# Stage two quantises its rows two tiles in advance, with the gate product on VectorE, and stage one forms four column sums and one row tile later

## The chip, the cores and the metric

The kernel runs on one core of one Trainium2 chip. A core has five engines that run side by side, each through its own list of instructions in a fixed order, and that meet only through semaphores: TensorE (PE in the profile; its weight loads are PEld), VectorE (DVE), ScalarE (ACT), GpSimd (POOL) and SyncE (SP, which here only issues transfers). The metric is the device time of one execution in microseconds (us). The kernel before takes 1054.46 us, the median of three runs that lie between 1053.47 and 1055.18 us.

## The reference, cut to what matters

An attention-like product and a SwiGLU feed-forward block, both on quantised numbers, over x of 2 x 1024 rows of 2048 features:

```python
x = x + matmul(fake_quant(layernorm(x)), fake_quant(ctx))     # 8 bits, one scale and zero point each
h = layernorm(x).astype(bfloat16)
qg, sg = dynamic_quant(h * inv_gate)     # scale of a row = max|.| / 127, then round to int8
qu, su = dynamic_quant(h * inv_up)
gate = (qg @ w_gate.T) * sg * s_gate     # w_gate, w_up: 1024 x 2048
up   = (qu @ w_up.T) * su * s_up
inter = clip(silu(gate) * up, -10, 10).astype(bfloat16)
qi, si = dynamic_quant(inter * inv_inter)
out = x + (qi @ w_down.T) * si * s_down  # w_down: 2048 x 1024
```

The zero points of the first product are brought in by sums: the column sums of the quantised context, times a constant, are added to every row (a column bias), and row sums of x come in at the very end. Each weight matrix is held as two fp16 halves, high and low, so that every product of the feed-forward block is two matmuls.

## The kernel before, in words

The 2048 rows are 16 row tiles of 128. There are three stages, and all matmuls are 128 x 128 by 128 x 512.

**Stage one** (line L1079) has 64 groups, each of one row tile m and one chunk of 512 context columns: 16 matmuls into one of five PSUM banks. There are four chunks for each of two batches, so eight chunks, 0 to 7, each of four quarters; the quarters are the 32 context transfers. A quarter is loaded into one of three staging buffers (ACT issues the load, L439), rounded to uint8 (VectorE, L762; the last quarter of each chunk ScalarE, L446), and cast to fp16 (ScalarE, L455; the last one GpSimd, L698). VectorE adds the four quarters of a chunk in fp16 (`col_add`, L779 and L782), TensorE sums the result over the partitions with a matrix of ones (`col_sum`, L1048, four matmuls), and ScalarE writes the bias (`col_bias`, L476). VectorE empties each group's bank into the row tile (`evacuate`, L808), GpSimd adds the column bias (`adjust`, L691), and SyncE stores the finished tile to a scratch tensor (`store_x2`). Row tiles 8 to 15 take over the memory of earlier ones: tile 13 is loaded when the last quarter, number 31, has been cast by GpSimd, and tile 15 when tile 8 has been stored. A row tile m is normalised and quantised (`ln1_stats` L789, `quantise_x` L462 and L470) and turned by a DMA transpose (`transpose_x`, L266) before its first group. The tables `adds_at`, `colsum_after`, `colbias_at`, `stats_at`, `quantise_at` say at which group number each engine does which of these; each engine walks through the 64 group numbers in order.

**Stage two** (L1099) has 64 jobs, one for each row tile t and one of four parts p: 0 and 2 are gate, 1 and 3 are up, 512 columns each; a job is 32 matmuls. A part's weights come in four granules of 1 MB, one transfer each. ScalarE takes their absolute sums (`w_abs`, L493), VectorE makes a power-of-two scale of them (`w_scale`, from L814), ScalarE writes the high half (`w_hi`, L507) and VectorE the low half (`w_lo`, L849), in turns. A job of part p waits for all low halves of that part. Of the first two row tiles a part is run for both before the next half's parts follow (tile 0 gate and up, tile 1 gate and up of the first 512 columns, then part 2 of both, then part 3 of both); the last two row tiles run half by half. For each row tile SyncE loads the 128 rows back (`load_x2`), VectorE takes their statistics (`ln2_stats`, L789), GpSimd makes the row scalars (`ln2_scalars`, from L663), ScalarE writes h in bf16 (`h_bf16`, L517), GpSimd multiplies h by inv_gate (`smooth_gate`, L672) and by inv_up (`smooth_up`, L684), VectorE finds the row maximum and rounds to int8 (`quantise`, L870 and L861), ScalarE casts to fp16 (`cast_q`, L529), and SyncE turns the result by a DMA transpose (`transpose_q`, L295) into one of two buffers for even and odd tiles. The results are emptied by VectorE (`evac_gate` L883, `evac_up` L891 to L898) with the silu on ScalarE between them (L535), then quantised for the third stage (`quant_inter`, L905 and on, `cast_qi` L539).

**Stage three** (L1111) has 64 products of 16 matmuls, one for each row tile and one of four output chunks, whose weights are parts 4 to 7 of two granules each; `down` (L920, L925) empties them.

The order is written by hand, engine by engine. In the middle of stage two VectorE's order for row tile t is this, one tile in advance:

```python
ln2_stats(t + 1)
evac_gate(t, 0)
quantise(0, t + 1)
evac_up(t, 0)
evac_gate(t, 1)
quantise(1, t + 1)
evac_up(t, 1)
quant_inter(t)
```

## Time and profile before

| what | value |
|---|---|
| median of three runs | 1054.46 us |
| the profiled execution, whole | 1058.52 us |
| its span on the core | 1056.8 us |
| TensorE busy | 939.6 us, 89% |
| VectorE busy | 666.1 us, 63% |
| ScalarE busy | 360.4 us, 34% |
| GpSimd busy | 295.3 us, 28% |

One profiled execution is the source of every row below. The part of the span in which an engine's instructions run is its busy time; what counts for the end is where TensorE, the busiest, does nothing, and what it then waits for. In rows of the timeline the first number is the start in the span, the second the length, and what stands in brackets is the idle time before the instruction and what ended it.

### The profile page before, as it was taken

To read this page: it belongs to the slowest core of one execution; us is meant where nothing else is said; L and a number is where in the kernel's file an instruction comes from. 1 tells how busy PE (TensorE), PEld (TensorE's weight loads), DVE (VectorE), ACT (ScalarE), POOL (GpSimd) and SP (SyncE) were. 2 spreads that over 40 slices of the span, in tenths; PEclk is the share of its full clock that TensorE was granted. 3 is DMA by queue.
4 is the path that set the end of the run, shared out by engine and by line. 5 is a ranking of instruction groups with operands and counts; after the bars stand their busy time and mean duration, and the time that the engine had idled before them with its cause. 6 is when DMAs were issued, how large, how long until landed. Compare 5 with 4: busy or idle time off the path is not lost.

```text
span 1056.8 us, 11253 instructions
## 1 busy us (share of the span) xinstructions
PE 939.6 (89%) x4192; PEld 416.0 (39%) x4192; DVE 666.1 (63%) x1006; ACT 360.4 (34%) x281; POOL 295.3 (28%) x256
## 2 busy tenths in 40 slices
PE   1689886799696778899999999999959989999998
PEld 1333332344242333344444444444424434444443
DVE  5469374657396777666777777777566694444443
ACT  4735456456445652222222333333226520000000
POOL 2226655364356021333333323223420000000000
PEclk9799988899897888899999999999989989999999
DMA  9665797976848803231333333333349630994112
GB/s 356 240 268 199 245 368 227 350 271 204 289 165 274 282 21 78 79 71 54 89 90 90 90 90 90 90 90 90 80 125 336 255 110 1 314 347 136 80 80 79
DMA packets 131686, 179.52 MB, mean 170 GB/s; under 512 B 111024, under 2 KB 111024, under 8 KB 113968
## 3 DMA queue, kind: packets, MB, share of 16 engines
q1 hardware_dynamic: 126848, 144.72, 43.8%
q10 hardware_dynamic: 4752, 34.08, 8.1%
q8 instruction: 33, 0.54, 0.2%
q0 software_dynamic: 32, 0.00, 0.1%
q14 instruction: 21, 0.17, 0.1%
HBM read 113.77 MB, written 37.75 MB: 143 GB/s over the span
## 4 chain that ended last, share of the span: by engine, by line
PE 58%; DVE 12%; issue 10%; DMA 8%; POOL 5%; ACT 5%; ACTq 0%; SPq 0%; DVEq 0%; POOLq 0%
PE ps L1099 36%; PE ps L1111 19%; DVE w_slots L849 5%; POOL x_tile L691 3%; PE ps L1079 3%; DMA ctx_stage<-in_ctx 2%; DVE small_operands L789 2%; DMA q1T<-x_q 2%; ACT x_i L462 1%; DMA w_raw<-in_w_gu 1%; DMA x_tile<-in_x 1%; DMA w_raw<-in_w_dn 1%; DVE ctx_u L762 1%; POOL ctx_slot L698 1%; DMA qT_odd<-q_f 1%
## 5 line engine op out<-in xcount | busy, mean ns | idle before, releaser
L1079 PE MATMUL ps<-ctx_slot,q1T 128*128 128x512 f16 x1024 | 237.2, 394 | 22.5 <-DMA q1T<-x_q 11.1
L1099 PE MATMUL ps<-w_slots,qT_even 128*128 128x512 f16 x1024 | 233.5, 391 | 21.1 <-issue 8.6
L1099 PE MATMUL ps<-w_slots,qT_odd 128*128 128x512 f16 x1024 | 231.9, 389 | 21.8 <-issue 19.7
L1111 PE MATMUL ps<-w_slots,qiT 128*128 128x512 f16 x1024 | 224.1, 382 | 4.1 <-DVE gate_and_up L891 4.1
L1079 PEld LDWEIGHTS ps<-ctx_slot,q1T 128*128 128x128 f16 x1024 | 102.7, 101 | 154.4 <-issue 16.8
L1099 PEld LDWEIGHTS ps<-w_slots,qT_even 128*128 128x128 f16 x1024 | 102.0, 100 | 151.8 <-issue 32.2
L1099 PEld LDWEIGHTS ps<-w_slots,qT_odd 128*128 128x128 f16 x1024 | 101.8, 100 | 151.2 <-issue 35.2
L1111 PEld LDWEIGHTS ps<-w_slots,qiT 128*128 128x128 f16 x1024 | 100.8, 99 | 127.3 <-DVE w_slots L849 4.6
L529 ACT ACTIVATE q_f<-q_i 128x2048 f16<-128x2048 int8 x32 | 61.1, 1910 | 195.0 <-DVE q_i L861 190.1
L920 DVE SCALAR_TENSOR_TENSOR down_tmp<-ps,small_operands,down_scales_b 128x512 f32<-128x512 f32 x64 | 48.0, 750 | 99.3 <-PE ps L1111 99.2
L870 DVE TENSOR_REDUCE small_operands<-x_and_xs 128x1 f32<-128x2048 f32 x19 | 43.4, 2284 | 105.9 <-POOL x_and_xs L672 102.3
L691 POOL TENSOR_TENSOR x_tile<-x_tile,col_bias 128x512 f32<-128x512 f32 x64 | 92.5, 1467 | 39.4 <-DVE x_tile L808 39.4
L808 DVE SCALAR_TENSOR_TENSOR x_tile<-ps,small_operands,x_tile 128x512 f32<-128x512 f32 x64 | 46.6, 734 | 57.1 <-PE ps L1079 56.9
L849 DVE SCALAR_TENSOR_TENSOR w_slots<-w_raw,small_operands,w_slots 128x1024 f16<-128x1024 f32 x48 | 68.7, 1430 | 13.9 <-ACT w_slots L507 10.4
L663 POOL TENSOR_SCALAR small_operands<-small_operands 128x1 f32<-128x1 f32 x16 | 4.0, 251 | 261.4 <-DVE small_operands L792 261.4
L672 POOL TENSOR_TENSOR x_and_xs<-h_bf,inv_gate_b 128x2048 f32<-128x2048 bf16 x16 | 65.5, 4092 | 39.2 <-ACT h_bf L517 39.2
L455 ACT ACTIVATE ctx_slot<-ctx_u 128x2048 f16<-128x2048 uint8 x24 | 45.5, 1905 | 74.4 <-DVE ctx_u L762 48.3
L507 ACT ACTIVATE w_slots<-w_raw,small_operands 128x1024 f16<-128x1024 f32 x48 | 52.4, 1139 | 30.2 <-DVE small_operands L832 17.4
L684 POOL TENSOR_TENSOR xs_up<-h_bf,inv_up_b 128x2048 f32<-128x2048 bf16 x13 | 53.2, 4096 | 0.0
L925 DVE SCALAR_TENSOR_TENSOR x_tile<-x_tile,small_operands,down_tmp 128x512 f32<-128x512 f32 x64 | 48.1, 752 | 2.3
L517 ACT ACTIVATE h_bf<-x_and_xs,small_operands 128x2048 bf16<-128x2048 f32 x15 | 31.4, 2093 | 53.0 <-POOL small_operands L666 53.0
L789 DVE BATCH_NORM_STATS2 small_operands<-x_and_xs 128x6 f32<-128x512 f32 x60 | 37.1, 681 | 8.7 <-DMA x_and_xs<-x_scratch 8.3
(91 smaller groups left out, 679.1 us busy)
## 6 DMA issues: line engine op xcount, KB each, us to landing
ctx_stage<-in_ctx ACTq DMA_DIRECT2D x32, 1024.0 KB, 8.1
x_scratch<-x_tile SPq DMA_DIRECT2D x16, 1024.0 KB, 5.0
w_raw<-in_w_gu SPq DMA_DIRECT2D x16, 1024.0 KB, 9.1
x_tile<-x_scratch SPq DMA_DIRECT2D x16, 1024.0 KB, 8.4
x_tile<-in_x SPq DMA_DIRECT2D x15, 1024.0 KB, 9.4
x_and_xs<-x_scratch SPq DMA_DIRECT2D x15, 1024.0 KB, 5.8
out_x<-x_tile SPq DMA_DIRECT2D x15, 1024.0 KB, 5.1
w_raw<-in_w_dn SPq DMA_DIRECT2D x8, 1024.0 KB, 9.2
```

Of the source, the lines that this page charges most:

```text
L507: nc.scalar.activation(hi[:, a * 2 * CW:(a + 1) * 2 * CW], raw[:, raw_unit(p, g), a * 2 * CW:(a + 1) * 2 * CW], ACT.Identity, bias=0.0, sc ...
L529: nc.scalar.activation(q16[:, :], q8[:, :], ACT.Copy).then_inc(q16_ready[which], 1)
L672: nc.gpsimd.tensor_tensor(bufA[:, :], hb[:, :], invg_b[:, :], ALU.mult).then_inc(xs_ready[0], 1)
L684: nc.gpsimd.tensor_tensor(dst[:, :], hb[:, :], invu_b[:, :], ALU.mult).then_inc(xs_ready[1], 1)
L691: nc.gpsimd.tensor_tensor(part, part, colb[:, j % 4, :], ALU.add).then_inc(adj_done, 1)
L789: ins = nc.vector.bn_stats(stats[:, 6 * c:6 * c + 6], src[:, c * CW:(c + 1) * CW])
L849: nc.vector.scalar_tensor_tensor(lo[:, cols], raw[:, raw_unit(p, g), cols], wsc[:, p:p + 1], hi[:, cols], ALU.mult, ALU.subtract).then_inc ...
L920: nc.vector.scalar_tensor_tensor(tmp[:, i % 2, :], ps[:, bank(S3 + i), :], si[:, t:t + 1], swd_b[:, c, :], ALU.mult, ALU.mult).then_inc(ev ...
L925: nc.vector.scalar_tensor_tensor(part, part, rterm[:, t:t + 1], tmp[:, i % 2, :], ALU.add, ALU.add).then_inc(res_done, 1)
L1079: last = nc.tensor.matmul(ps[:, bank(g), :], q1T[m][:, k, :], ctx_s[j % 4][:, k, :], start=(k == 0), stop=(k == KT - 1))
L1099: last = nc.tensor.matmul(ps[:, bank(S2 + i), :], qT[t % 2][:, which, k, :], wsl[:, unit(p, k // 4), hl, k % 4, :], start=(k == 0 and hl = ...
L1111: last = nc.tensor.matmul(ps[:, bank(S3 + i), :], qiT[t % 8][:, k, :], wsl[:, unit(4 + c, k // 4), hl, k % 4, :], start=(k == 0 and hl == ...
```

## The change

Four things change. The column sums of chunks 4 to 7 stand three groups later on TensorE, and VectorE makes the three additions of each of these chunks together instead of one after each quarter. The order of the groups of row tiles 13, 14 and 15 is another one:

```diff
-        groups += [(12, c) for c in range(NCH)] + [(13 + g % 3, g // 3) for g in range(12)]
+        groups += [(12, c) for c in range(NCH)]
+        for half in ((0, 1), (2, 3)):
+            groups += [(m, c) for c in half for m in (13, 14)] + [(15, c) for c in half]
...
-        adds_at.update({g + 1: (q,) for g, q in quad_at.items() if g >= 20})
+        adds_at.update({4 * j + 9: (4 * j + 1, 4 * j + 2, 4 * j + 3) for j in range(4, 8)})
...
-        colsum_after = {6: 0, 9: 1, 11: 2, 14: 3, 25: 4, 29: 5, 33: 6, 37: 7}
-        colbias_at = {7: 0, 10: 1, 12: 2, 15: 3, 26: 4, 30: 5, 34: 6, 38: 7}
+        colsum_after = {6: 0, 9: 1, 11: 2, 14: 3, 28: 4, 32: 5, 36: 6, 40: 7}
+        colbias_at = {7: 0, 10: 1, 12: 2, 15: 3, 29: 4, 33: 5, 37: 6, 41: 7}
```

On TensorE, in the groups of the second half of the first batch and the beginning of the second, where `q1T` is a turned row tile, `ctx_slot` a context chunk and `ones` the matrix of a column sum, this stands before:

```order
L1079 MATMUL ps<-ctx_slot2_53,q1T5_79 128x512 x16
L1048 MATMUL ps<-ctx_colacc_93,ones_133 128x512 x4
L1079 MATMUL ps<-ctx_slot2_53,q1T6_80 128x512 x16
L1079 MATMUL ps<-ctx_slot2_53,q1T7_81 128x512 x16
L1079 MATMUL ps<-ctx_slot3_54,q1T4_78 128x512 x16
L1079 MATMUL ps<-ctx_slot3_54,q1T5_79 128x512 x16
L1048 MATMUL ps<-ctx_colacc_93,ones_133 128x512 x4
```

and this after:

```order
L1084 MATMUL ps<-ctx_slot2_53,q1T5_79 128x512 x16
L1084 MATMUL ps<-ctx_slot2_53,q1T6_80 128x512 x16
L1084 MATMUL ps<-ctx_slot2_53,q1T7_81 128x512 x16
L1084 MATMUL ps<-ctx_slot3_54,q1T4_78 128x512 x16
L1053 MATMUL ps<-ctx_colacc_93,ones_133 128x512 x4
L1084 MATMUL ps<-ctx_slot3_54,q1T5_79 128x512 x16
```

The column sum of chunk 4 has moved behind three more groups; those of chunks 5, 6 and 7 move in the same way. At the end of stage one TensorE has this before, in which `q1T15` is row tile 15:

```order
L1079 MATMUL ps<-ctx_slot0_51,q1T13_87 128x512 x16
L1079 MATMUL ps<-ctx_slot0_51,q1T14_88 128x512 x16
L1079 MATMUL ps<-ctx_slot0_51,q1T15_89 128x512 x16
L1079 MATMUL ps<-ctx_slot1_52,q1T13_87 128x512 x16
L1079 MATMUL ps<-ctx_slot1_52,q1T14_88 128x512 x16
```

and this after:

```order
L1084 MATMUL ps<-ctx_slot0_51,q1T13_87 128x512 x16
L1084 MATMUL ps<-ctx_slot0_51,q1T14_88 128x512 x16
L1084 MATMUL ps<-ctx_slot1_52,q1T13_87 128x512 x16
L1084 MATMUL ps<-ctx_slot1_52,q1T14_88 128x512 x16
L1084 MATMUL ps<-ctx_slot0_51,q1T15_89 128x512 x16
```

Row tile 15 comes in for the first time as the 57th group instead of the 55th.

Third, the gate product moves from GpSimd to VectorE, where it stands at the head of `quantise(0, t)`; GpSimd keeps the up product:

```diff
             for t in range(2, NT):
                 ln2_scalars(t)
-                smooth_gate(t)
                 smooth_up(t)
```

Fourth, from row tile 2 on stage two quantises row tile t + 2 while t is computed, where it was t + 1. VectorE's list gains the product and the loop changes; at the beginning the fourth low half of part 1 goes behind the first quantisation, and at the end the last emptying of stage two goes ahead of the weights of parts 6 and 7:

```diff
+            def smooth_gate(t):
+                dve.wait_ge(hb_ready, t + 1)
+                if t == 0:
+                    dve.wait_ge(invg_in, 16)
+                if t in (1, 2):
+                    dve.wait_ge(q8_written, q8_at["u", t - 1] + 1)
+                nc.vector.tensor_tensor(bufA[:, :], hb[:, :], invg_b[:, :], ALU.mult).then_inc(xs_ready[0], 1)
+
             def quantise(which, t):
+                if which == 0:
+                    smooth_gate(t)
...
-                if 56 <= g < 60:
-                    w_lo(1, g - 56)
+                if g in (56, 57, 58, 60):
+                    w_lo(1, {56: 0, 57: 1, 58: 2, 60: 3}[g])
...
-                if g == 60:
+                if g == 59:
                     quantise(0, 0)
...
-            for t in range(2, NT - 2):
-                ln2_stats(t + 1)
+            for t in range(2, NT - 1):
                 evac_gate(t, 0)
-                quantise(0, t + 1)
+                if t + 2 < NT:
+                    ln2_stats(t + 2)
                 evac_up(t, 0)
-                evac_gate(t, 1)
-                quantise(1, t + 1)
-                if t == NT - 3:
-                    ln2_stats(NT - 1)
-                    quantise(0, NT - 1)
-                evac_up(t, 1)
-                quant_inter(t)
-            evac_gate(NT - 2, 0)
-            quantise(1, NT - 1)
-            evac_up(NT - 2, 0)
+                if t + 2 < NT:
+                    evac_gate(t, 1)
+                    quantise(0, t + 2)
+                    evac_up(t, 1)
+                    quant_inter(t)
+                    quantise(1, t + 2)
             evac_gate(NT - 1, 0)
             evac_up(NT - 1, 0)
...
             evac_up(NT - 2, 1)
             quant_inter(NT - 2)
+            evac_gate(NT - 1, 1)
+            evac_up(NT - 1, 1)
+            quant_inter(NT - 1)
             w_scale(6)
             sw_scale(6)
             w_lo(6, 0)
             w_lo(6, 1)
-            evac_gate(NT - 1, 1)
-            w_scale(7)
-            sw_scale(7)
-            w_lo(7, 0)
-            w_lo(7, 1)
-            evac_up(NT - 1, 1)
-            quant_inter(NT - 1)
             dve.wait_ge(rterm_ready, 1)
             for i in range(G1):
+                if i == 6:
+                    w_scale(7)
+                    sw_scale(7)
+                    w_lo(7, 0)
+                    w_lo(7, 1)
                 down(i)
```

ScalarE follows, with the casts of the next rows ahead of the silu:

```diff
-            for t in range(2, NT - 2):
-                h_bf16(t + 1)
-                silu(t, 0)
-                cast_q(0, t + 1)
-                silu(t, 1)
-                cast_q(1, t + 1)
...
+            for t in range(3, NT):
+                cast_q(0, t)
+                cast_qi(t - 2)
+                cast_q(1, t)
+                silu(t - 1, 0)
+                if t + 1 < NT:
+                    h_bf16(t + 1)
+                    silu(t - 1, 1)
```

and so does SyncE:

```diff
-            for t in range(2, NT - 2):
-                store_qi(t - 1)
-                transpose_q(0, t + 1)
-                load_x2(t + 2)
-                transpose_q(1, t + 1)
+            for t in range(3, NT):
+                if t + 1 < NT:
+                    load_x2(t + 1)
+                transpose_q(0, t)
+                store_qi(t - 2)
+                if t + 1 < NT:
+                    transpose_q(1, t)
```

Here is a turn of VectorE's loop up to the first emptying of an up job. `x_and_xs` is the buffer of the loaded rows and of the gate product, `q_i` the int8 result, L883 and L891 the emptying of gate and up. Before:

```order
L883 SCALAR_TENSOR_TENSOR gate_and_up<-ps,small_operands,gate_up_scales_b 128x512
L870 TENSOR_REDUCE small_operands<-x_and_xs 128x1
L871 TENSOR_SCALAR small_operands<-small_operands 128x1
L874 COPY small_operands<-small_operands 128x1
L856 RECIPROCAL small_operands<-small_operands 128x1
L861 TENSOR_SCALAR q_i_104<-x_and_xs,small_operands 128x2048
L891 SCALAR_TENSOR_TENSOR gate_and_up<-ps,small_operands,gate_up_scales_b 128x512
```

After:

```order
L886 SCALAR_TENSOR_TENSOR gate_and_up<-ps,small_operands,gate_up_scales_b 128x512
L862 TENSOR_TENSOR x_and_xs<-h_bf_103,inv_gate_b 128x2048
L873 TENSOR_REDUCE small_operands<-x_and_xs 128x1
L874 TENSOR_SCALAR small_operands<-small_operands 128x1
L877 COPY small_operands<-small_operands 128x1
L849 RECIPROCAL small_operands<-small_operands 128x1
L854 TENSOR_SCALAR q_i_104<-x_and_xs,small_operands 128x2048
L894 SCALAR_TENSOR_TENSOR gate_and_up<-ps,small_operands,gate_up_scales_b 128x512
```

The product (L862) is new on VectorE, and the emptying ahead of it is now that of part 2 of the tile, where it was part 0.

At the beginning of stage two the weights of parts 2 and 3 are prepared in another order. On ScalarE, where `abs_junk` marks an absolute sum, `w_slots` a high half (two instructions to a granule) and `gate_and_up` a silu, this stands before:

```order
L493 ACTIVATE abs_junk_late_112,small_operands_135<-w_raw_49 128x2048
L507 ACTIVATE w_slots_50<-w_raw_49,small_operands_135 128x1024 x8
L493 ACTIVATE abs_junk_late_112,small_operands_135<-w_raw_49 128x2048 x3
L535 ACTIVATE gate_and_up_106<-gate_and_up_106 128x512
L507 ACTIVATE w_slots_50<-w_raw_49,small_operands_135 128x1024 x8
```

and this after:

```order
L508 ACTIVATE w_slots_50<-w_raw_49,small_operands_135 128x1024 x4
L536 ACTIVATE gate_and_up_106<-gate_and_up_106 128x512
L494 ACTIVATE abs_junk_late_112,small_operands_135<-w_raw_49 128x2048
L508 ACTIVATE w_slots_50<-w_raw_49,small_operands_135 128x1024 x2
L494 ACTIVATE abs_junk_late_112,small_operands_135<-w_raw_49 128x2048
L508 ACTIVATE w_slots_50<-w_raw_49,small_operands_135 128x1024 x2
```

Part 2's eight high halves stood together; now its last four have two absolute sums of part 3 among them. In this beginning SyncE stores row tiles 13 to 15 after more of the weight loads and after the transpose of the first up rows, and loads part 3 in the order of its granules.

## Rows read from the trace of the kernel before

**Rows 1.** Page, part 1: busy time of the engines, share, instructions.

```profile
PE 939.6 (89%) x4192; PEld 416.0 (39%) x4192; DVE 666.1 (63%) x1006; ACT 360.4 (34%) x281; POOL 295.3 (28%) x256
```

**Rows 2.** What TensorE waited for: total us, times, longest.

```profile
PE ps L1048 <- DVE ctx_colacc L782: 21.9, 6, 8.1
```

**Rows 3.** Timeline of TensorE in stage one: start, length, operation, wait before.

```profile
151.28 1.89 PE L1048 MATMUL ps<-ctx_colacc,ones 128*128 128x512 f16 x4 [4.74 <-DVE ctx_colacc L782]
...
176.24 1.89 PE L1048 MATMUL ps<-ctx_colacc,ones 128*128 128x512 f16 x4 [8.09 <-DVE ctx_colacc L782]
...
197.88 1.89 PE L1048 MATMUL ps<-ctx_colacc,ones 128*128 128x512 f16 x4 [5.29 <-DVE ctx_colacc L782]
...
216.86 1.04 PE L1048 MATMUL ps<-ctx_colacc,ones 128*128 128x512 f16 x4 [1.52 <-DVE ctx_colacc L782]
217.74 55.42 PE L1079 MATMUL ps<-ctx_slot,q1T 128*128 128x512 f16 x256
281.21 36.62 PE L1079 MATMUL ps<-ctx_slot,q1T 128*128 128x512 f16 x160 [8.06 <-DMA q1T<-x_q]
```

**Rows 4.** Timelines of VectorE, GpSimd and ScalarE in stage one.

```profile
174.96 1.23 DVE L782 TENSOR_TENSOR ctx_colacc<-ctx_colacc,ctx_slot 128x2048 f16<-128x2048 f16 x1 [4.06 <-POOL ctx_slot L698]
...
265.50 2.46 DVE L789 BATCH_NORM_STATS2 small_operands<-x_tile 128x6 f32<-128x512 f32 x4
...
212.60 1.90 POOL L698 TENSOR_SCALAR ctx_slot<-ctx_u 128x2048 f16<-128x2048 uint8 x1 [8.31 <-ACT ctx_u L446]
...
225.41 1.91 ACT L493 ACTIVATE abs_junk_early<-w_raw 128x2048 uint8<-128x2048 f32 x1 [12.90 <-DMA w_raw<-in_w_gu]
```

**Rows 5.** Windows: PE, PEld, DVE, ACT, POOL busy, clock, DMA share, GB/s.

```profile
120.00:210.00 90.00, 69.68 (x293) 29.88 (x294) 51.34 (x60) 45.69 (x30) 41.64 (x39) 0.89 0.94 320
```

**Rows 6.** Timeline of TensorE at the beginning of stage two.

```profile
323.99 9.77 PE L1099 MATMUL ps<-w_slots,qT_even 128*128 128x512 f16 x32 [6.17 <-DMA qT_even<-q_f]
337.80 9.69 PE L1099 MATMUL ps<-w_slots,qT_even 128*128 128x512 f16 x32 [4.04 <-issue]
351.58 9.63 PE L1099 MATMUL ps<-w_slots,qT_odd 128*128 128x512 f16 x32 [4.09 <-issue]
...
392.14 9.84 PE L1099 MATMUL ps<-w_slots,qT_even 128*128 128x512 f16 x32 [6.28 <-DVE w_slots L849]
...
420.32 23.20 PE L1099 MATMUL ps<-w_slots,qT_even 128*128 128x512 f16 x96 [4.54 <-issue]
446.82 30.51 PE L1099 MATMUL ps<-w_slots,qT_odd 128*128 128x512 f16 x128 [3.30 <-issue]
477.17 27.79 PE L1099 MATMUL ps<-w_slots,qT_even 128*128 128x512 f16 x128
```

**Rows 7.** Timelines of VectorE, GpSimd and ScalarE at the beginning of stage two.

```profile
306.66 6.39 DVE L849 SCALAR_TENSOR_TENSOR w_slots<-w_raw,small_operands,w_slots 128x1024 f16<-128x1024 f32 x2 [1.47 <-ACT w_slots L507]
...
381.12 10.95 DVE L849 SCALAR_TENSOR_TENSOR w_slots<-w_raw,small_operands,w_slots 128x1024 f16<-128x1024 f32 x8
...
448.67 1.23 DVE L905 TENSOR_TENSOR gate_and_up<-inter_even,inv_inter_b 128x1024 f32<-128x1024 bf16 x1
...
305.66 4.10 POOL L672 TENSOR_TENSOR x_and_xs<-h_bf,inv_gate_b 128x2048 f32<-128x2048 bf16 x1
...
368.84 1.91 ACT L493 ACTIVATE abs_junk_late<-w_raw 128x2048 uint8<-128x2048 f32 x1
```

**Rows 8.** Window in the middle of stage two, and VectorE there.

```profile
500.00:600.00 100.00, 100.00 (x463) 44.86 (x462) 73.18 (x110) 30.41 (x23) 28.95 (x22) 1.00 0.38 95
...
521.15 2.29 DVE L870 TENSOR_REDUCE small_operands<-x_and_xs 128x1 f32<-128x2048 f32 x1 [7.20 <-POOL x_and_xs L672]
```

**Rows 9.** Timeline of TensorE at the end of stage two.

```profile
779.72 8.90 PE L1099 MATMUL ps<-w_slots,qT_odd 128*128 128x512 f16 x32 [11.05 <-issue]
789.87 7.07 PE L1099 MATMUL ps<-w_slots,qT_odd 128*128 128x512 f16 x32 [1.25 <-issue]
...
852.88 199.79 PE L1111 MATMUL ps<-w_slots,qiT 128*128 128x512 f16 x912 [4.14 <-DVE gate_and_up L891]
```

More of the change, by code:

```diff
@@ L581, in _ @@
             cast_q(0, 1)
+            silu(0, 0)
             w_abs(2, 2)
@@ L623, in _ @@
             cast_qi(NT - 2)
[L624 to L632 removed]
+            w_abs(6, 0)
+            w_abs(6, 1)
+            silu(NT - 1, 1)
+            w_abs(7, 0)
+            w_abs(7, 1)
+            cast_qi(NT - 1)
+            for p in (6, 7):
+                w_hi(p, 0)
+                w_hi(p, 1)
         @block.gpsimd
@@ L719, in _ @@
                     adjust(n)
-            smooth_gate(1)
             for n in adjust_at[G1]:
```

95 lines of the change are left out of this document (41 added, 54 removed).

## The prediction

> **What bounds the kernel now.** I read the shares of the engines first: TensorE is busy 939.6 of 1056.8 us, no other engine over 666.1 [rows 1]. So the time is TensorE's work plus 117 us in which it stands still, and some further work done at the lower of its two clock levels after it stood. Then I read its timeline for every stop, and at each one who ends it.
>
> In the middle of stage two there is none: a window of 100 us is 100 us busy at a granted clock of 1.00, that is 2.4 GHz [rows 8], and one row tile of four jobs takes 27.79 us [rows 6]. The same holds in stage three. Whatever the change does to other engines there is worth nothing unless it makes them slower than 27.8 us for a row tile. The stops lie in four places. In stage one TensorE waits before four column sums, 4.74, 8.09, 5.29 and 1.52 us [rows 3], most of the 21.9 us that it waits for these sums in all [rows 2], and later 8.06 us for the transpose of row tile 15 [rows 3]. At the beginning of stage two come waits of 6.17, 4.04, 4.09, 6.28, 4.54 and 3.30 us [rows 6]; those marked "issue" end when a DMA transpose of quantised rows lands, the one with w_slots when the low halves of a part are ready. At the end of it come 11.05 and 1.25 us for the last transposes, and in stage three 4.14 us for the last emptying, which stands on VectorE behind weight work [rows 9].
>
> A stop costs more than its length. 32 matmuls take 27.79 / 4 = 6.95 us at 2.4 GHz; behind a stop they take 9.77, 9.69 or 9.84 [rows 6], since part of them runs at 1.2 GHz. That is 2.7 to 2.9 us on top of each stop of 3 us or more.
>
> **The change part by part.** A positive number is time saved.
>
> *A. Column sums, 10.* Starts of these four sums lie 25.0, 21.6 and 19.0 us apart [rows 3], while four groups take 4 x 55.42 / 16 = 13.9. So the stream of context quarters, not the place of the sum, sets this pace, and a sum moved back by three groups only lets TensorE run ahead by 10.4 us. What follows does not hang on TensorE: GpSimd's cast of the last quarter at 212.60 releases a row tile load and the first weights, for which ScalarE then waits 12.90 us [rows 4]. If the stream keeps its pace, TensorE will give its lead back by waiting for banks, because VectorE's emptying stands behind the scale of part 0's weights. So only what the stream itself gains counts. It gains this: before, VectorE waited 4.06 us with the addition of a chunk's last quarter (1.23) while the next chunk's first rounding stood behind it [rows 4]. Now the additions come one group later, behind that rounding. That is 5.3 us at one chunk boundary; I take the same at the next, 10.6, and call it 10. Bounds: 0, if the stream is held elsewhere, and 19.6, the four waits. The transfers leave some room, but not much: 0.94 of the DMA engines' time between 120 and 210 us, at 320 GB/s [rows 5].
>
> *B. Row tile 15, 6.9.* Its first group comes two groups later, 2 x 3.46 us. Since its statistics (265.50 before, [rows 4]) stay tied to the chain of A, the end of stage one comes 6.9 nearer to that chain. The wait itself shrinks by less, because TensorE also arrives with what is left of its lead from A, some 5 us; about 6 of it stay. Bounds 0 and 8.1.
>
> *C. First transpose of stage two, 3.5.* Row tile 0 is loaded when row tile 15's first group is done, now with 7 groups behind it instead of 9, which costs 6.9 of cover. Against that, the chain loses the fourth low half of part 1, 6.39 us ahead of the first maximum [rows 7], and the gate product gets shorter: VectorE makes 128x1024 of the same types in 1.23 us, so twice that, 2.4, against 4.10 on GpSimd [rows 7]. The gap becomes 6.17 + 6.9 - 6.4 - 1.7 = 5.0. VectorE also comes to the statistics earlier, as the scale of part 1 no longer has to wait behind a late emptying; for this I take half of the 5.0, so 6.17 - 2.5, about 3.5 saved. Bounds -2 and 6.2.
>
> *D. The rest of the beginning, 8.* From the first job at 323.99 to the fifth row tile at 477.17 TensorE needs 153.2 us for 16 jobs of 6.95, so 42 are lost. With rows ready two tiles ahead the last two waits go, 4.54 + 3.30, and their low clock (23.20 - 3 x 6.95 = 2.4 and 30.51 - 27.79 = 2.7): 12.9. Half of the 4.09 goes as well, 2.0, because the second gate rows no longer queue behind stores. But part 2's last two granules now have two absolute sums of 1.91 [rows 7] among them on ScalarE, and VectorE's low halves, and with them part 2's first job, come 3.8 us later; a stop there makes the clock fall, 2.8 more. 12.9 + 2.0 - 6.6 = 8.3, taken as 8. What now is late next at this place is the low halves of parts 2 and 3, not the rows. Bounds -7 (only the new waits) and 42; I take the value at the low end because the weight work (eight low halves alone 10.95 us [rows 7]) stays.
>
> *E. The end of stage two, 19.6.* The last rows are quantised a whole row tile before TensorE asks for them, so 11.05 goes, and with it the low clock, 8.90 - 6.95 = 2.0. With the last emptying ahead of parts 6 and 7, the 4.14 go, and the low clock behind them: 199.79 - 912 x 55.42 / 256 = 2.4. The 1.25 I leave out. Weights of parts 4 and 5 have five jobs, 35 us, from their load on, and stage three then comes to part 6 after 12 products and to part 7 after 18, so these hide. Bounds 0 and 21.
>
> *F. VectorE's new load, 0.* Per row tile it is busy 73.18 x 27.79 / 100 = 20.3 us, and waited 7.20 us for the gate product [rows 8]. The wait goes, 2.4 come in: 22.7, under 27.8. TensorE's work covers this; the cover is 5.1 us per row tile.
>
> Here is what speaks against F. While GpSimd made a product of 4.10 us, two low halves took VectorE 6.39 us; eight undisturbed ones take 10.95, so 1.4 each [rows 7], and the two lost 3.7. Both products of a row tile are now released by the same h, so the gate product can start just behind GpSimd's and lose up to 4.1. The Trainium skill, "SBUF — State Buffer", section "SBUF: two separate sides", says the same as a rule: a VectorE instruction with two SBUF inputs and a GpSimd instruction share one port pair, whichever starts first holds it throughout, the other is blocked entirely. The trace agrees with 6.39 against 2.7. By this the load is 22.7 + 4.1 = 26.8, still under 27.8, and the sum stays.
>
> Sum: 10 + 6.9 + 3.5 + 8 + 19.6 = 48.0 us. Against the profiled execution's own 1058.5 that is 1010.5; that execution is 4.1 above the median of the runs, so I predict 1054.5 - 48.0 = 1006.5 us.
>
> **The rivals.** *The stream keeps its pace* (A is 0): the 0.94 of DMA time [rows 5] speaks for it, since transposes and stores share these engines; the waiting rounding behind 4.06 us speaks against. 1016.5 us. *The weights decide the beginning* (D is -7): parts 2 and 3 are scaled later than now, and every later low half too; the wait of 6.28 for w_slots shows that they already do once [rows 6]. 1021.5 us. *The end keeps its stop* (E is 0): transposes come in time, but TensorE reaches stage three before part 4 is ready; against it stand the five jobs of cover. 1026 us. *VectorE becomes the bound of stage two, slower than before*: with colliding products it is at 26.8 us, and if its roundings and inter products are blocked by the up product as well, or each silu is waited for, it passes 27.8. It pays per row tile, in twelve of them: at 33 us, 12 x 5.2 = 62 us, so 1006.5 + 62 = 1068. It only outweighs the gain from 27.8 + 48 / 12 = 31.8 us on, 5 above the collided load, for which no row speaks.
>
> **How the numbers follow.** Differences under 0.2%, about 2 us, can't be told from none here. Forecast 0.64, with a range of its own from 998 to 1014; stream 0.16; weights 0.12; end 0.04; VectorE 0.04. Only the last ends slower, and nothing lies near zero, but 0.02 I keep for gains and new waits that cancel: faster 0.94, same 0.02, slower 0.04. The range goes down to 992, where A is nearly 20 and D some 13, and up to 1026, which takes in the first three rivals.
>
> **What would show it.** A: GpSimd's last cast of a context quarter near 202 instead of 212.6; no stops before column sums over 4 us; instead short waits of TensorE for emptied banks near row tile 12. B and C: TensorE's first job of stage two near 303, a wait of some 6 us left at row tile 15 and one under 4 before the first job. D: waits for w_slots before parts 2 and 3 of about 8 us, then none from row tile 2 on. E: no stop over 1 us from there to the last matmul, and the first product of stage three about 35 us after row tile 15's first job. F: VectorE about 80% busy in the middle with TensorE at 100%. The forecast is wrong if GpSimd's last cast hardly moves, if a stop appears in every row tile of stage two, or if stage three waits for low halves.

## The result and the profile after

The changed kernel takes 1012.67 us (median of 4 runs, 1008.1 to 1020.4) against 1054.82 for the kernel before (1053.47 to 1059.44); the ratio is 0.9598, 95% interval 0.9564 to 0.9632. It is 42 us faster, where 48 were forecast. The profiled execution took 1015.74 us with a span of 1014.0, 42.8 under the span before. The ratios here and below leave out slow executions, of which there were two: 1024.24 us (the changed kernel, taken again) and 1023.65 us (both edits to ScalarE's order together).

Part 1 of its page answers to [rows 1]: TensorE's busy time falls by 26 us with the same 4192 matmuls, while its mean granted clock rises from 0.950 to 0.976, so less of this work ran at the lower clock. VectorE's busy time rises by 41 us.

```profile
PE 913.8 (90%) x4192; PEld 410.0 (40%) x4192; DVE 707.3 (70%) x1022; ACT 361.4 (36%) x281; POOL 252.5 (25%) x240
```

TensorE's timeline of stage one (start, length, operation, wait before) answers to [rows 3]. L1053 are the column sums of chunks 4 to 7, and the last line begins with row tile 15. The first long run of groups is put ahead here, that of the kernel before (L1079) and then the changed kernel's.

```profile
122.19 24.35 PE L1079 MATMUL ps<-ctx_slot,q1T 128*128 128x512 f16 x112 [2.77 <-DMA q1T<-x_q]
```

```profile
119.06 34.71 PE L1084 MATMUL ps<-ctx_slot,q1T 128*128 128x512 f16 x160 [2.76 <-DMA q1T<-x_q]
153.60 1.03 PE L1053 MATMUL ps<-ctx_colacc,ones 128*128 128x512 f16 x4
...
189.15 1.86 PE L1053 MATMUL ps<-ctx_colacc,ones 128*128 128x512 f16 x4 [20.21 <-ACT col_bias L477]
...
205.70 1.03 PE L1053 MATMUL ps<-ctx_colacc,ones 128*128 128x512 f16 x4
...
220.38 1.03 PE L1053 MATMUL ps<-ctx_colacc,ones 128*128 128x512 f16 x4
221.24 51.96 PE L1084 MATMUL ps<-ctx_slot,q1T 128*128 128x512 f16 x240
278.47 29.39 PE L1084 MATMUL ps<-ctx_slot,q1T 128*128 128x512 f16 x128 [5.27 <-DMA q1T<-x_q]
```

Four stops of together 19.6 us have become one of 20.2. All column sums use one PSUM bank, so col_sum(5) waits until ScalarE has read col_sum(4) out of it (col_bias(4)). GpSimd's and ScalarE's timelines answer to [rows 4]: the stream's last cast came at 208.2 (before 212.6, forecast 202). As the long run of groups began 3.1 us earlier, the stream itself gained only 1.3 of these 4.4 us. ScalarE's first work on the weights comes 14.1 us behind that cast (before 12.8).

```profile
208.21 2.93 POOL L694 TENSOR_SCALAR ctx_slot<-ctx_u 128x2048 f16<-128x2048 uint8 x1 [3.57 <-ACT ctx_u L447]
...
222.32 1.91 ACT L494 ACTIVATE abs_junk_early<-w_raw 128x2048 uint8<-128x2048 f32 x1 [13.63 <-DMA w_raw<-in_w_gu]
```

TensorE's timeline at the beginning and end of stage two answers to [rows 6, 9]. The waits for late rows at row tiles 2 and 3 fell from 4.54 and 3.30 to 1.11 and 0.66, the one for part 3's low halves grew from 6.28 to 9.13, and from row tile 4 on there is no stop at all. A wait of 2.99 for part 2's low halves is new.

```profile
312.67 8.63 PE L1104 MATMUL ps<-w_slots,qT_even 128*128 128x512 f16 x32 [4.81 <-DVE x_tile L801]
326.65 8.46 PE L1104 MATMUL ps<-w_slots,qT_even 128*128 128x512 f16 x32 [5.36 <-issue]
338.09 7.07 PE L1104 MATMUL ps<-w_slots,qT_odd 128*128 128x512 f16 x32 [2.97 <-issue]
...
361.26 7.08 PE L1104 MATMUL ps<-w_slots,qT_even 128*128 128x512 f16 x32 [2.99 <-DVE w_slots L842]
...
384.37 8.63 PE L1104 MATMUL ps<-w_slots,qT_even 128*128 128x512 f16 x32 [9.13 <-DVE w_slots L842]
...
407.92 20.88 PE L1104 MATMUL ps<-w_slots,qT_even 128*128 128x512 f16 x96 [1.11 <-issue]
429.45 27.93 PE L1104 MATMUL ps<-w_slots,qT_odd 128*128 128x512 f16 x128 [0.66 <-issue]
457.23 27.79 PE L1104 MATMUL ps<-w_slots,qT_even 128*128 128x512 f16 x128
...
733.49 13.98 PE L1104 MATMUL ps<-w_slots,qT_even 128*128 128x512 f16 x64
...
788.74 221.18 PE L1116 MATMUL ps<-w_slots,qiT 128*128 128x512 f16 x1024
```

The window in the middle answers to [rows 8]; VectorE has 84 us of 100 where it had 73.

```profile
500.00:600.00 100.00, 100.00 (x465) 45.32 (x464) 84.08 (x116) 31.75 (x23) 26.29 (x20) 1.00 0.34 89
```

In the kernel before, row tile 14, with which the end of stage two begins, started here:

```profile
754.69 13.97 PE L1099 MATMUL ps<-w_slots,qT_even 128*128 128x512 f16 x64
```

From these rows the 42.8 us split by place. The first long run of groups began at 119.06 and not at 122.19: 3.1, in work that the change does not touch; in the other kernels tried, which share that code, it began between 119.3 and 122.3, so this is chance. From there to the end of stage one (307.86, before 317.83) it took 188.8 for 195.6: 6.8. From there to row tile 4's first job 149.4 for 159.3: 10.0. The ten row tiles 4 to 13 276.3 for 277.5: 1.3. From there to the end 280.5 for 302.1: 21.6.

### The profile page after: what moved, and what is told of

It is laid out like the page before. It is cut to its first block, busy times and chain, and to the rows that moved or that the text cites. A ratio compares the mean times of both kernels' runs of the same rounds, so it can differ in the third digit from the quotient of the medians.

```text
span 1014.0 us, 11256 instructions
## 1 busy us (share of the span) xinstructions
PE 913.8 (90%) x4192; PEld 410.0 (40%) x4192; DVE 707.3 (70%) x1022; ACT 361.4 (36%) x281; POOL 252.5 (25%) x240
## 4 chain that ended last, share of the span: by engine, by line
PE 67%; DMA 11%; DVE 9%; issue 6%; ACT 3%; POOL 2%; SPq 1%; ACTq 0%; DVEq 0%; POOLq 0%
PE ps L1104 40%; PE ps L1116 22%; PE ps L1084 5%; DMA q1T<-x_q 5%; DMA ctx_stage<-in_ctx 2%; DVE w_slots L842 2%; DMA w_raw<-in_w_gu 2%; DVE small_operands L782 2%; DVE ctx_u L755 1%; POOL x_tile L687 1%; DMA small_operands<-in_params 1%; ACT x_q L471 1%; DMA qT_odd<-q_f 1%; SPq L297 1%; DVE small_operands L873 1%
## 5 line engine op out<-in xcount | busy, mean ns | idle before, releaser
L1104 PE MATMUL ps<-w_slots,qT_even 128*128 128x512 f16 x1024 | 227.6, 385 | 23.4 <-DVE w_slots L842 12.1
L1084 PE MATMUL ps<-ctx_slot,q1T 128*128 128x512 f16 x1024 | 231.1, 387 | 18.0 <-DMA q1T<-x_q 8.3
L1104 PE MATMUL ps<-w_slots,qT_odd 128*128 128x512 f16 x1024 | 224.8, 381 | 8.0 <-DVE w_slots L842 4.4
L1116 PE MATMUL ps<-w_slots,qiT 128*128 128x512 f16 x1024 | 221.2, 379 | 0.0
L687 POOL TENSOR_TENSOR x_tile<-x_tile,col_bias 128x512 f32<-128x512 f32 x64 | 101.4, 1608 | 35.6 <-DVE x_tile L801 35.6
L680 POOL TENSOR_TENSOR xs_up<-h_bf,inv_up_b 128x2048 f32<-128x2048 bf16 x13 | 63.7, 4902 | 28.7 <-ACT h_bf L518 28.7
L886 DVE SCALAR_TENSOR_TENSOR gate_and_up<-ps,small_operands,gate_up_scales_b 128x512 f32<-128x512 f32 x32 | 23.9, 748 | 43.0 <-PE ps L1104 42.7
L755 DVE TENSOR_SCALAR ctx_u<-ctx_stage,small_operands 128x2048 uint8<-128x2048 f32 x24 | 38.3, 1595 | 16.3 <-DMA ctx_stage<-in_ctx 11.5
L862 DVE TENSOR_TENSOR x_and_xs<-h_bf,inv_gate_b 128x2048 f32<-128x2048 bf16 x16 | 43.2, 2703 | 8.4 <-ACT h_bf L518 8.4
```

What stands on the lines that cost most here:

```text
L680: nc.gpsimd.tensor_tensor(dst[:, :], hb[:, :], invu_b[:, :], ALU.mult).then_inc(xs_ready[1], 1)
L687: nc.gpsimd.tensor_tensor(part, part, colb[:, j % 4, :], ALU.add).then_inc(adj_done, 1)
L755: nc.vector.tensor_scalar(cu8[:, q % 2, :, :], stage[q % 3][:, :, :], is2[:, 0:1], qp[:, 3:4], ALU.mult, ALU.add).then_inc(c_quant, 1)
L1084: last = nc.tensor.matmul(ps[:, bank(g), :], q1T[m][:, k, :], ctx_s[j % 4][:, k, :], start=(k == 0), stop=(k == KT - 1))
L1104: last = nc.tensor.matmul(ps[:, bank(S2 + i), :], qT[t % 2][:, which, k, :], wsl[:, unit(p, k // 4), hl, k % 4, :], start=(k == 0 and hl = ...
L1116: last = nc.tensor.matmul(ps[:, bank(S3 + i), :], qiT[t % 8][:, k, :], wsl[:, unit(4 + c, k // 4), hl, k % 4, :], start=(k == 0 and hl == ...
```

## The experiments

Each kernel was timed in rounds with the kernel before on the same chip; ratios are to that, and spans and rows are of one profiled execution. "Stage one" is the time from the start of its first long run of groups (near 120 us) to the end of its last.

### The column sums put back

```diff
-        adds_at.update({4 * j + 9: (4 * j + 1, 4 * j + 2, 4 * j + 3) for j in range(4, 8)})
+        adds_at.update({g + 1: (q,) for g, q in quad_at.items() if g >= 20})
-        colsum_after = {..., 28: 4, 32: 5, 36: 6, 40: 7}
+        colsum_after = {..., 25: 4, 29: 5, 33: 6, 37: 7}
```

(colbias_at likewise.) 

> The changed kernel with the three tables of the column sums (when the quarters are added, after which group the sum is taken, when its bias is formed) put back to those of the kernel before. Theory: moving the sums gave nothing, since one stop of 20.2 us before col_sum(5) took the place of four that came to 19.6 us: 1011 to 1015 us (the changed kernel has 1012.7), and the four stops before column sums are back, 4 to 8 us each. Rival, the prediction's first term: the move was worth 10 us and something else ate it: 1021 to 1025 us.

Measured: 1019.06 us, 0.9626 (0.9610 to 0.9643); all its runs between 1018.4 and 1019.2. The four stops are back (4.74, 9.55, 4.64 and 4.91 us):

```profile
148.44 1.89 PE L1053 MATMUL ps<-ctx_colacc,ones 128*128 128x512 f16 x4 [4.74 <-DVE ctx_colacc L775]
...
174.26 1.89 PE L1053 MATMUL ps<-ctx_colacc,ones 128*128 128x512 f16 x4 [9.55 <-DVE ctx_colacc L775]
...
218.93 91.99 PE L1084 MATMUL ps<-ctx_slot,q1T 128*128 128x512 f16 x416
```

That is 3 us behind the changed kernel's 0.9598, with intervals that overlap: over all executions the move is not worth 10 us. The time lies above the 1011 to 1015 expected, but this chip's kernel before is 4 us slower too; by the ratio it would be 1015 us beside the changed kernel's first four. Stage one took 191.6 us, from 119.36 to 310.92.

### The bias earlier, the rounding earlier, both

The first moves col_bias(4) on ScalarE from group 29 to 26, the second changes one number, the third is both.

```diff
+                if g == 26:
+                    col_bias(4)
-        quantise_at = {..., 24: 9, 26: 10, 28: 11, ...}
+        quantise_at = {..., 24: 9, 27: 10, 28: 11, ...}
```

> The changed kernel, ScalarE forms col_bias(4) at group 26 and not at group 29, so that col_sum(5) does not wait for it behind three casts and a row tile. Theory: what holds TensorE there is the context stream and the transposed row tile 11, which landed at 196.1 us, 1.7 us before TensorE came to need it: the one stop of 20.2 us falls apart into a stop of about 10 us (for the sum of chunk 5, whose last quarter is added at 178.6 us) and one of about 7 us (row tile 11), total 1010 to 1013 us. Rival: the wait for the bias alone lost the prediction's 10 us: 1001 to 1005 us and no stop over 10 us left there.

Measured: 1019.53 us (1009.8 to 1022.9), 0.9612 (0.9579 to 0.9645): no gain. The profiled execution (1022.87) had long transposes, 14.2 and 15.3 us for row tiles 8 and 9. In it TensorE's long stop only fell apart, as the theory had it, into the wait for the sum itself and one for row tile 11's transpose:

```profile
184.55 1.89 PE L1055 MATMUL ps<-ctx_colacc,ones 128*128 128x512 f16 x4 [12.25 <-DVE ctx_colacc L777]
...
199.23 8.60 PE L1086 MATMUL ps<-ctx_slot,q1T 128*128 128x512 f16 x32 [4.71 <-DMA q1T<-x_q]
```

So in that execution the wait that I had overlooked is what one sees, and not what bounds.

> The changed kernel, ScalarE rounds the context's quarter 23 before it quantises row tile 10 and not behind it. In the changed kernel the second half of that quantisation waited 7.1 us for the transpose of row tile 9, and the rounding stood behind it. Theory: the rounding starts near 165.5 us (174.5 in the changed kernel), GpSimd's cast and the scalars of row tile 11 with it, row tile 11 lands near 190 us (196.1), col_bias(4) is formed near 183 us (188.3), and the total is 1007 to 1009 us. Rival: the stop belongs to the moved column sums alone, and the order on ScalarE before it is worth nothing: 1011 to 1014 us.

Measured: 1015.9 us (1007.6 to 1018.8), 0.9591 (0.9563 to 0.9619), not told apart from the changed kernel. In the profiled execution (1007.63) the rounding of quarter 23 started at 160.6, the long stop was 11.83 and stage two began at 304.9; but there the transposes of row tiles 8 and 9 had taken 8.3 and 9.3 us, so that execution cannot say what the order did.

> Both edits together: col_bias(4) at group 26, and the rounding of quarter 23 ahead of row tile 10 on ScalarE. Theory (stream and row tile 11 hold TensorE, each edit takes one of two waits that follow one another): the stop before col_sum(5) shrinks to about 4 us, the group of row tile 11 starts near 190 us (197.8 in the changed kernel), total 1004 to 1007 us. Rival (the bias alone): as the kernel with the bias early, 1001 to 1005 us, and the two differ by less than 1 us.

Measured: 1011.72 us (1008.3 to 1023.7), 0.9558 (0.9528 to 0.9589); the interval overlaps the changed kernel's. The sum no longer waits; the transposes of row tiles 10 and 11 do the holding (1.94 and 10.39 us), and the group of tile 11 starts at 190.7, near the 190 expected. Its shortest executions, 1008.3 and 1008.4, are no shorter than the changed kernel's:

```profile
170.21 1.04 PE L1055 MATMUL ps<-ctx_colacc,ones 128*128 128x512 f16 x4 [0.22 <-DVE ctx_colacc L777]
...
176.64 3.63 PE L1086 MATMUL ps<-ctx_slot,q1T 128*128 128x512 f16 x16 [1.94 <-DMA q1T<-x_q]
190.66 9.07 PE L1086 MATMUL ps<-ctx_slot,q1T 128*128 128x512 f16 x32 [10.39 <-DMA q1T<-x_q]
```

### The changed kernel again

> The changed kernel as it is, for a second profile of it and for a time on the same chip as the three beside it. Theory: what differs from execution to execution is how long the transposes of row tiles 8 and 9 take beside the context loads (14.0 and 14.1 us in the first profile): where they take 7 to 10 us, the rounding of quarter 23 starts before 168 us, the stop before col_sum(5) is under 16 us, and stage two begins before 308 us; where they take 14 us, all is as in the first profile (20 us, 312.7 us). Ratio to the kernel before 0.956 to 0.963. Rival: the stop of 20 us is there with short transposes as well.

Measured: 1020.82 us, 0.9605 (0.9555 to 0.9656). With the first four there are ten times of this kernel: four from 1008.1 to 1009.6 and six from 1015.7 to 1024.2. The granted clock does not part them: its means are 0.972 to 0.975 in the four and 0.966 to 0.976 in the six. Below they are called the lower and the upper group. The profiled one (1021.43) belongs to the upper group: the two transposes took 13.8 and 16.0 us, and the stop 22.4.

```profile
192.70 1.87 PE L1053 MATMUL ps<-ctx_colacc,ones 128*128 128x512 f16 x4 [22.43 <-ACT col_bias L477]
...
225.73 51.96 PE L1084 MATMUL ps<-ctx_slot,q1T 128*128 128x512 f16 x240
```

### Only the order of row tiles 13 to 15

The kernel before, with the change's new lines for `groups` alone.

> The kernel before with one edit of the change alone: the order of the groups of row tiles 13 to 15, so that two more groups stand ahead of row tile 15's first. Theory (the prediction's term of 6.9 us): the stop of 8.06 us before row tile 15's first group falls to 0.5 to 2 us, stage one ends 6 to 7 us earlier, and the total falls by 5 to 8 us, ratio 0.992 to 0.995. Rival: stage two's beginning waits for weights and for row tile 0 that come no earlier, and the total falls by less than 2 us, ratio over 0.998.

Measured: 1051.1 us, 0.9929 (0.9905 to 0.9953), 7.5 us (5 to 10) faster. The profiled span, 1051.4, is 5.4 shorter. Stage one takes 187.5 us for 195.6. TensorE then waits 10.00 us for row tile 0's transposed rows, where it had waited 6.17 [rows 6]: about half of stage one's gain is lost again at once, since row tile 0's chain has two groups less in front of it.

```profile
120.36 24.35 PE L1081 MATMUL ps<-ctx_slot,q1T 128*128 128x512 f16 x112 [2.77 <-DMA q1T<-x_q]
...
280.02 27.80 PE L1081 MATMUL ps<-ctx_slot,q1T 128*128 128x512 f16 x128 [1.42 <-DMA q1T<-x_q]
317.82 8.41 PE L1101 MATMUL ps<-w_slots,qT_even 128*128 128x512 f16 x32 [10.00 <-DMA qT_even<-q_f]
```

### The old order at the end of stage two

As before, ScalarE forms part 6's high halves ahead of `silu(NT - 1, 1)` and part 7's behind it, ahead of `cast_qi(NT - 1)`. VectorE empties the last gate job behind part 6's weights and the last up job behind part 7's (VectorE's part of the edit):

```diff
-            evac_gate(NT - 1, 1)
-            evac_up(NT - 1, 1)
-            quant_inter(NT - 1)
             w_scale(6)
             sw_scale(6)
             w_lo(6, 0)
             w_lo(6, 1)
+            evac_gate(NT - 1, 1)
+            w_scale(7)
+            ...
+            evac_up(NT - 1, 1)
+            quant_inter(NT - 1)
```

> The changed kernel with ScalarE's and VectorE's order at the end of stage two put back to the kernel before's (weights of parts 6 and 7 between the last row tiles' emptying), while rows are still quantised two tiles in advance. Theory (the prediction split the end's 19.6 us into 13.05 us from the advance and 6.5 us from this order): 5 to 8 us slower than the changed kernel, ratio 0.964 to 0.970, with a stop of some 4 us before stage three's products. Rival: the advance alone takes all of it, and the time is the changed kernel's within 2 us.

Measured: 1023.66 us, 0.9657 (0.9615 to 0.9698), some 5 us behind the changed kernel on the same chip, with intervals that overlap a little. The rows are sharper: from stage three's first product to the end it took 233.0 us, with the changed kernel 225.3, so this order is worth 7.7. The 11 us stop [rows 9] did not come back; it belongs to the advance.

```profile
811.66 199.13 PE L1115 MATMUL ps<-w_slots,qiT 128*128 128x512 f16 x912 [5.42 <-DVE gate_and_up L894]
```

### The bank of group 60 first

```diff
-                if g in (56, 57, 58, 60):
+                if g in (56, 57, 58, 61):
```

(the last low half of part 1 moves with it.) 

> The changed kernel, VectorE forms the last low half of part 1 (7.0 us beside GpSimd) one group later, so that the bank of group 60 is emptied ahead of it and stage two's first job need not wait for it. Theory: the first job starts 2 us earlier (at its transposed rows' landing), but the second waits for the same quantised up rows as before, so the 2 us become a longer wait there and the time stays: within 1 us of the changed kernel. Rival (the prediction's third term taken as a place on the path): 2 us faster.

Measured: 1008.04 us (1006.7 to 1021.7), 0.9560 (0.9510 to 0.9609). The first job starts 1.7 us behind the end of stage one and not 4.8, but the second waits 8.29 for 5.36, and starts 17.0 us behind that end. In kernels that have the changed kernel's code up to there it was 17.4 (the old end order), 18.7 and 18.8 (the changed kernel's two). By row tile 4's first job the distance from the end of stage one is 148.2, there 148.1, 149.7 and 149.4. So of the first job's 3.1 us at most 1.5 are left at row tile 4; the lower median comes from four of six executions in the lower group.

```profile
301.89 7.07 PE L1104 MATMUL ps<-w_slots,qT_even 128*128 128x512 f16 x32 [1.67 <-DVE w_slots L842]
317.25 9.33 PE L1104 MATMUL ps<-w_slots,qT_even 128*128 128x512 f16 x32 [8.29 <-issue]
```

This kernel's stage one is the changed kernel's, instruction for instruction, up to group 60, and its profiled execution is of the lower group. ScalarE's timelines of the two beside each other show where the groups part. L447 rounds quarters 19 and 23, L471 is the second half of a row tile's quantisation. First the changed kernel, then this one:

```profile
142.13 2.08 ACT L447 ACTIVATE ctx_u<-ctx_stage,small_operands 128x2048 uint8<-128x2048 f32 x1
...
156.37 1.91 ACT L471 ACTIVATE x_q<-x_i 128x2048 f16<-128x2048 int8 x1 [2.39 <-DMA q1T<-x_q]
...
172.56 1.91 ACT L471 ACTIVATE x_q<-x_i 128x2048 f16<-128x2048 int8 x1 [7.08 <-DMA q1T<-x_q]
...
174.47 2.08 ACT L447 ACTIVATE ctx_u<-ctx_stage,small_operands 128x2048 uint8<-128x2048 f32 x1
```

```profile
142.36 2.08 ACT L447 ACTIVATE ctx_u<-ctx_stage,small_operands 128x2048 uint8<-128x2048 f32 x1
...
154.25 1.91 ACT L471 ACTIVATE x_q<-x_i 128x2048 f16<-128x2048 int8 x1
...
165.29 1.91 ACT L471 ACTIVATE x_q<-x_i 128x2048 f16<-128x2048 int8 x1 [3.18 <-DMA q1T<-x_q]
...
167.20 2.08 ACT L447 ACTIVATE ctx_u<-ctx_stage,small_operands 128x2048 uint8<-128x2048 f32 x1
```

Row tile 9 may be written to the one buffer x_q only when row tile 8's transpose has read it, row tile 10 only behind row tile 9's, and the rounding of the stream stands behind both. Windows show the transfers in that time (PE, PEld, DVE, ACT, POOL busy, clock, DMA share, GB/s), again changed kernel first: the DMA engines are as busy in both, and move a third in the execution of the upper group. Most of that lies in four of the seven us: from 152 to 156 the changed kernel moved 81 GB/s, this one 358.

```profile
149.00:156.00 7.00, 7.00 (x35) 3.14 (x33) 6.76 (x10) 3.18 (x2) 6.33 (x6) 1.00 1.19 109
```

```profile
149.00:156.00 7.00, 7.00 (x35) 3.11 (x33) 6.76 (x10) 5.17 (x3) 6.40 (x6) 1.00 1.04 360
```

The other traces agree. Of the eleven profiled executions with the column sums moved, six have a transpose of row tile 8 or 9 that took 13.8 us or more, and their stage one took 188.8 to 193.6 us; in the other five none took over 10.3, and stage one took 178.9 to 183.8. In the three executions profiled with the sums at their old place these transposes took 6.5 to 10.4 us. Whether moving the sums brings the long transposes about is not shown.

### The loads behind the transpose

```diff
-                    if ahead < QUADS and (kq < 2 or ahead % 4 != 2):
+                    if ahead not in (22, 23) and ahead < QUADS and (kq < 2 or ahead % 4 != 2):
                         load_quad(ahead)
...
+                if m == 9:
+                    load_quad(22)
+                    load_quad(23)
                 nc.scalar.activation(xq[:, :], xi8[:, :], ACT.Copy, ...)
```

> The changed kernel, ScalarE issues the loads of the context's quarters 22 and 23 once row tile 8's transpose has landed (it waits there for that anyway) and not 5 us after that transpose was issued. Theory: what parts the executions of the changed kernel, near 1009 and near 1020 us on this chip, is whether row tile 8's transpose takes 8 or 14 us, and it takes 14 only where these loads are issued into it: the transpose takes 7 to 9 us, the rounding of quarter 23 starts 24 to 27 us after that of quarter 19, and five of six times lie between 1005 and 1013 us. Rival: the long transposes come from elsewhere, and the times fall in both groups as before; or the later loads delay the stream as much as they spare it, and all lie near 1014 us.

Measured: 1020.58 us, 0.9641 (0.9611 to 0.9672), all six between 1016.8 and 1023.4. Row tile 8's transpose took 8.6 us as expected; but the loads now met row tile 9's, and it took 16.8 (view of the DMA issues: copies, median us from issue to landing):

```profile
q1T<-x_q SPq DMA_TRANSPOSE x1, 16.8
```

The rounding of quarter 23 came 33.5 us behind that of quarter 19, as in the upper group. The theory is half fallen: without these loads row tile 8's transpose was short, but they met the next one. Loads beside a transpose do not settle it alone either, since with group 60 first the two met as well and it took 8.3 us.

> Four edits together on the changed kernel: the loads of quarters 22 and 23 behind row tile 8's transpose, quarter 23's rounding ahead of row tile 10, col_bias(4) at group 26, and the last low half of part 1 behind the emptying of group 60. Theory: the stream is held by nothing but the loads, stage two starts near 302 us in every execution, 1003 to 1008 us. Rival: TensorE is bound there by row tile 11 and by the weights, which follow the loads, and it is no faster than the kernel with the late loads alone, within 2 us.

Measured: 1019.94 us, 0.9631 (0.9602 to 0.9661): no gain. This kernel has four edits: the loads behind the transpose, the bias earlier, the rounding earlier and the bank of group 60 first. Row tile 9's transpose took 20.4 us, and TensorE, which no longer waits for the bias, waits for row tiles 9, 10 and 11 in turn:

```profile
178.09 6.50 PE L1089 MATMUL ps<-ctx_slot,q1T 128*128 128x512 f16 x16 [4.00 <-DMA q1T<-x_q]
188.03 4.96 PE L1089 MATMUL ps<-ctx_slot,q1T 128*128 128x512 f16 x16 [3.44 <-DMA q1T<-x_q]
198.04 8.53 PE L1089 MATMUL ps<-ctx_slot,q1T 128*128 128x512 f16 x32 [5.05 <-DMA q1T<-x_q]
```

### VectorE's load and the gate product's place

The maximum of the gate rows is taken twice from row tile 3 on:

```diff
+                for _ in range(2 if t >= 3 and which == 0 else 1):
                     link(nc.vector.tensor_reduce(amax, buf[:, :], ...
```

> The changed kernel with the maximum of the gate rows (2.29 us) taken twice from row tile 3 on, so that VectorE has 2.4 us more in each row tile of stage two. Theory (the prediction's sixth term, VectorE has 22.7 us of work in a period of 27.6 us): the period stays 27.6 us, and the time is the changed kernel's within 3 us. Rival: VectorE's order is itself the chain that TensorE follows, and the period grows by 2.4 us, 31 us in all (13 row tiles), 1040 to 1050 us.

Measured: 1019.6 us (1011.1 to 1026.2), 0.9620 (0.9573 to 0.9667), not told apart from the changed kernel. VectorE is at 91 of 100 us, which is 2.0 us more in a row tile, TensorE still at 100, the period still 27.6. Two short stops appear all the same, 3.54 us before row tile 3, where the changed kernel had 0.66, and 1.25 before row tile 15's second job:

```profile
436.07 27.96 PE L1105 MATMUL ps<-w_slots,qT_odd 128*128 128x512 f16 x128 [3.54 <-issue]
```

```profile
500.00:600.00 100.00, 100.00 (x465) 45.35 (x464) 91.18 (x124) 32.48 (x24) 28.07 (x21) 1.00 0.40 95
```

The last kernel gives `smooth_gate` back to GpSimd, ahead of `smooth_up`, and keeps the advance.

> The changed kernel with the gate product back on GpSimd (4.1 us each beside 3.4 us and 2.3 us on VectorE), rows still quantised two tiles in advance. Theory: the place of the product is worth little in the middle, where nothing waits for it, and 2 to 5 us at the beginning of stage two, where the first rows wait for both products in turn: 1 to 6 us slower than the changed kernel, period 27.6 us. Rival: the advance cannot be kept up with both products on GpSimd (8.2 us and the scalars, beside VectorE's use of the same memory), TensorE stops in each row tile, and it is more than 10 us slower.

Measured: 1019.5 us, 0.9642 (0.9604 to 0.9680), some 4 us behind the changed kernel, intervals overlapping. Its period is 27.6 as well, and its way from row tile 4 to the end no longer; but from the end of stage one to row tile 4 it takes 154.1 us for 149.4. The product's new place pays at the beginning of stage two alone.

## Why the prediction was right, and where it was off

The forecast (1006.5, range 992 to 1026) names the right places and, but for A, the right mechanism. A was too large, and part of the nearness is luck: in the profiled execution A and B together fell short by 10.1 us and C and D by 1.5, while 3.1 of chance at the start, 1.3 in the middle that no term names and 2.0 more at the end came in.

**A, column sums, 10: this step failed in most executions.** The stream does gain about what was said, but only where the transposes are short: there the roundings of quarters 23, 27 and 31 follow at 24.8, 16.2 and 15.3 us (142.36, 167.20, 183.44, 198.76 with group 60 first) where before it was 25.0, 20.6 and 19.0, so 8.2 us instead of 10.6, and the last cast came at 200.95, near the 202 forecast. In the upper group the first distance is 32.3 to 34.1, and everything is lost. With the sums at their old place and the new order of groups, stage one took 187.5 us (that order alone) and 191.6 (the sums put back), one execution each. With the sums moved it took 188.8 and 192.3 in the changed kernel's two profiled executions and 191.0 with the maximum taken twice, all with long transposes, and 180.9, 182.5 and 183.8 in three kernels with short ones that share its code there but for the last groups (group 60 first, the old end order, the gate product on GpSimd). So A is 4 to 11 us where the transposes are short and nothing certain where they are long; over all executions it is 0 to 3 us, by ratios whose intervals overlap. I had costed the stream at VectorE and left out ScalarE, on which the rounding stands behind two transposes; and I had not seen that col_sum(5) waits for col_bias(4). The picture of TensorE was wrong in both groups: it gives its lead back not in short waits for banks but before col_sum(5), 20.21 and 22.43 us in the changed kernel and 13.22 in the execution with group 60 first. The rival of a stream that keeps its pace (0.16, 1016.5 us), for which 0.94 of DMA time spoke, is what happened in six of ten executions of the changed kernel.

**B, row tile 15, 6.9.** Stage one became 8.2 us shorter with this edit alone, in one profiled execution of each kernel; 5.27 us of wait stayed in the changed kernel, "about 6" was said.

**C and D, 11.5 together.** 10.0 measured. From the end of stage one to the first job it was 6.17 and is 4.81, so C is 1.4 (3.5 forecast); from there to row tile 4 it was 153.2 and is 144.6, so D is 8.6 (8 forecast). C's place hardly counts: the second job waits for the quantised up rows of row tile 0 in any case, and of 3.1 us taken from the first job at most 1.5 were left at row tile 4. D holds with its signs: the waits at row tiles 2 and 3 nearly went, part 3's grew. That part 2's and 3's waits would be near 8 us each was wrong for part 2: 2.99 and 9.13. The low clock behind a stop, 2.7 to 2.9 us in the sum, was smaller in this execution: 1.5 to 1.7 behind the stops of 4.81, 5.36 and 9.13 and 0.1 behind those of 2.97 and 2.99.

**E, the end, 19.6.** 21.6 measured, in the two pieces as named: the order 7.7 (6.5 forecast), the advance the rest, 13.9 (13.05 forecast). No kernel put the advance back alone, so its part is read from the stops that are gone and not from an experiment. The sign was miscounted: stage three's first product comes 41.4 us, six jobs, behind row tile 15's first job, and not 35.

**F, 0.** VectorE has 84.08 x 27.63 / 100 = 23.2 us in a row tile (22.7 forecast), and with 2.0 us more the period did not move, though a stop of 3.54 us came at row tile 3. The cover is there in the steady part. The rivals of weights, end and VectorE did not come true.

By the places the sum is 6.8 for A and B (16.9 forecast), 10.0 for C and D, 1.3 for the middle, 21.6 for E, and 3.1 of chance at the start. Executions of the lower group, 1008.1 to 1009.6, come within some 3 us of the forecast; the median lies above it, as most executions lose A.

None of the kernels tried is shown to be faster than the changed one: the lowest ratios, 0.9558 and 0.9560, have intervals that overlap its 0.9598 and 0.9605.

## What to carry to other kernels

Before costing a wait that an edit removes, list all semaphores of the waiting instruction, and all that stand ahead of the releaser on its own engine: the stop that shows is the last of several, and taking it away (the bias) uncovers the next. Rows made two tiles ahead removed the stop at the end of stage two and nearly all of those at row tiles 2 and 3; the steady part, which had none before, still has none with VectorE at 84 of 100 us, and none at 91. Much of what was left lay where transfers of different kinds meet. When times of one kernel fall in two groups, profile both before believing a median.

## What was not expected of the hardware

A DMA transpose of 128x2048 fp16 landed in 4.3 to 4.5 us by itself. Those of row tiles 8 and 9, among the context loads of 1 MB, landed in 6.5 to 10.4 us in some executions and in 13.8 to 16.0 in others; with two loads issued later it was up to 16.8 and 20.4. In one of the long ones the DMA engines showed a share of 1.19 and moved 109 GB/s. What decides between the two is open: the same issue order gave both.

Two products that start within 0.05 us on GpSimd and VectorE do not share: who is first keeps its own length, the other takes nearly the sum of both. Timelines of the changed kernel, GpSimd first at 412 us (VectorE 6.21 instead of 2.28), VectorE first at 437 (GpSimd 6.20 instead of 4.09). This is what the Trainium skill, "SBUF — State Buffer", section "SBUF: two separate sides", states of the shared port pair.

```profile
411.97 6.21 DVE L862 TENSOR_TENSOR x_and_xs<-h_bf,inv_gate_b 128x2048 f32<-128x2048 bf16 x1 [2.28 <-ACT h_bf L518]
437.40 2.29 DVE L862 TENSOR_TENSOR x_and_xs<-h_bf,inv_gate_b 128x2048 f32<-128x2048 bf16 x1 [1.42 <-ACT h_bf L518]
```

```profile
411.95 4.09 POOL L680 TENSOR_TENSOR xs_up<-h_bf,inv_up_b 128x2048 f32<-128x2048 bf16 x1 [2.21 <-ACT h_bf L518]
437.45 6.20 POOL L680 TENSOR_TENSOR xs_up<-h_bf,inv_up_b 128x2048 f32<-128x2048 bf16 x1 [2.21 <-ACT h_bf L518]
```
